# Two small products of a pair-representation kernel moved onto the two 64-row halves of the TensorE array

## The reference, cut to what matters

```python
# layer 0
xn = layernorm(x); left = sigmoid(xn@left1) * (xn@left2); right = sigmoid(xn@right1) * (xn@right2)
p  = layernorm(einsum('nsre,nkre->nske', left, right))
x1 = x + (p^T @ out_w) * sigmoid(xn @ gate)
# layer 1
left  = x1 @ W_left + b_left + x1 @ W_eq + b_eq
rsum  = sum(x1 @ W_right + b_right, axis=2)
o     = left * rsum * sigmoid(x1 @ W_gate + b_gate)
out   = layernorm(o @ W_out + b_out + x1)
```

## Time and profile before

| what | value |
|---|---|
| median of 3 runs | 123.48 us |
| the profiled execution's own time | 123.37 us |
| its span in the trace | 121.6 us |
| PE busy | 93.8 us (77%) |
| weight loads (PEld) busy | 71.7 us (59%) |
| DVE busy | 92.1 us (76%) |
| ACT busy | 73.6 us (61%) |
| POOL busy | 68.9 us (57%) |

### The profile page before, as it was taken

One profiled execution on the slowest core, in us unless ns is written; L12 is line 12 of the kernel. 1 busy time (PEld: TensorE's weight loads), 2 busy tenths in 40 slices (PEclk: granted clock), 3 DMA queues, 4 the chain that ended last, 5 costly groups with the idle time before them and its releaser, 6 DMA issues.

```text
span 121.6 us, 1791 instructions
## 1 busy us (share of the span) xinstructions
PE 93.8 (77%) x566; PEld 71.7 (59%) x566; DVE 92.1 (76%) x222; ACT 73.6 (61%) x129; POOL 68.9 (57%) x81
## 2 busy tenths in 40 slices
PE   1965795199879969999192999999999999697000
PEld 1954353067647759954141559897798879596000
DVE  1079999499988872999999636477498989799920
ACT  2245472976997628994136983645998698761100
POOL 5047679606299001790470397958754797995700
PEclk9999999968999999999998599999999999999755
DMA  2799990000000000000000000000000005429796
GB/s 52 137 147 153 144 129 3 0 0 0 5 0 0 0 3 5 0 3 0 0 0 0 0 0 5 0 0 3 0 0 5 0 0 86 66 35 145 109 145 104
DMA packets 33484, 4.51 MB, mean 37 GB/s; under 512 B 33348, under 2 KB 33476, under 8 KB 33476
## 3 DMA queue, kind: packets, MB, share of 16 engines
q1 hardware_dynamic: 32160, 4.06, 23.9%
q10 hardware_dynamic: 1316, 0.35, 1.4%
HBM read 2.31 MB, written 2.10 MB: 36 GB/s over the span
## 4 chain that ended last, share of the span: by engine, by line
PE 41%; DVE 35%; issue 7%; ACT 7%; DMA 4%; DVEq 0%; SPq 0%
PE bank L878 7%; PE bank L966 6%; DVE acc_p L713 6%; PE bank L1009 5%; PE bank L1018 4%; DMA x_tok<-in_x 4%; DVE lr L613 4%; PE bank L980 3%; PE bank L983 3%; PE bank L981 3%; DVE sums L584 3%; PE bank L939 3%; DVE lr L797 3%; ACT sig_lr L435 2%; DVE st L592 2%
## 5 line engine op out<-in xcount | busy, mean ns | idle before, releaser
L878 PE MATMUL bank<-lr_blk,xnT 64*128 64x256 f32 x128 | 20.1, 451 | 5.6 <-DVE lr L613 4.0
L878 PEld LDWEIGHTS bank<-lr_blk,xnT 64*128 64x128 f32 x128 | 13.3, 211 | 9.9 <-ACT xnT L425 5.4
L613 DVE TENSOR_TENSOR lr<-bank,sig_lr 128x512 f32<-128x512 f32 x16 | 15.8, 1045 | 2.9 <-ACT sig_lr L435 2.6
L363 POOL TENSOR_TENSOR x_low<-x1T,x_high 128x512 fp32r<-128x512 f32 x8 | 11.0, 1373 | 12.2 <-ACT x_high L496 12.1
L355 POOL TENSOR_TENSOR t_tok<-p_sb,rstd 128x512 f32<-128x512 f32 x7 | 10.4, 1489 | 4.9 <-DVE rstd L754 4.9
L414 ACT ACTIVATE std<-st,eps 128x16 f32<-128x16 f32 (+4 forms) x14 | 4.4, 318 | 13.6 <-DVE st L599 5.3
L279 POOL TENSOR_TENSOR xc<-x_tok,sums 128x512 f32<-128x512 f32 (+2 forms) x7 | 8.0, 1145 | 7.4 <-DVE sums L577 7.4
L435 ACT ACTIVATE sig_lr<-bank 128x512 f32<-128x512 f32 x16 | 9.5, 599 | 3.9 <-PE bank L878 3.8
L379 POOL TENSOR_TENSOR sq<-lr,row_rep 128x512 f32<-128x512 f32 x7 | 9.8, 1400 | 2.0 <-DVE lr L800 2.0
L966 PE MATMUL bank<-tT,out_blk 128*128 128x512 f32 x16 | 9.2, 659 | 2.2 <-DVE x1T L771 2.2
L371 POOL TENSOR_TENSOR oT<-o_a,rsum 128x512 f32<-128x512 f32 x8 | 8.7, 1088 | 2.6 <-issue 1.9
(11 more groups left out here) (120 smaller groups left out, 244.1 us busy)
## 6 DMA issues: line engine op xcount, KB each, us to landing
x_tok<-in_x SPq DMA_DIRECT2D x14, 128.0 KB, 4.3
out<-sq SPq DMA_DIRECT2D x7, 256.0 KB, 3.3
x_tok<-in_x SPq DMA_DIRECT2D x4, 64.0 KB, 4.4
w_rep<-in_weights ACTq DMA_DIRECT2D x1, 180.5 KB
out<-sq ACTq DMA_DIRECT2D x1, 128.0 KB, 4.6
out<-sq SPq DMA_DIRECT2D x1, 128.0 KB, 4.9
row_rep<-in_rows ACTq DMA_DIRECT2D x1, 32.0 KB, 5.0
```

Source lines behind the costliest of these rows:

```text
L363: nc.gpsimd.tensor_tensor(x1_low[:, c % 2], x1T[:, c % 3], x1_high[:, c % 2], ALU.subtract).then_inc(x1_low_ready, 1)
L613: nc.vector.tensor_tensor(lr[:, :, s].rearrange("p f s -> p s f"), src[:, :, 2 * CH:4 * CH], sig_lr[:, j % 3].rearrange("p (s f) -> p s f" ...
L878: last = nc.tensor.matmul(dst, xnT[half, c, k * P:(k + 1) * P], lr_blk[half].rearrange("p g m c -> p g (m c)"), start=True, stop=True, ski ...
```

## The change

`centre_y` and `project_y` are cut into halves by rows of the array. Each 128-row call becomes two calls of 64 rows: the upper 64 partitions of the data against the upper left 64 x 64 block of the matrix, and the lower 64 against the lower right one (the other two blocks are zero). The two halves write 64 columns each into two different banks, into the left 256 columns of each bank. So one chunk of y takes half of both banks 6 and 7, and the next chunk takes the same halves: there is one set of banks where there were two. `centre_y(c)` therefore waits until `evacuate_y(c-1)` has finished, where it waited for `evacuate_y(c-2)`. In the loop `centre_y(i-3)` stands behind `project_1(i-2)`, directly ahead of `project_y(i-3)`, where it stood ahead of `project_1(i-2)`. `evacuate_y` reads both banks in each of its two instructions, with the same 512 elements per partition. `project_scaled` is as before.

```diff
+        def y_place(t, j):
+            n, h = divmod(j, 2)
+            return bank[:, Y + t, 0:COLS // 2].rearrange("p (h g n c) -> p h n g c", h=2, g=2, n=2)[:, h, n]
...
             def evacuate_y(c):
                 s = slice(c * SPC, (c + 1) * SPC)
-                src = bank[:, Y + c % 2].rearrange("p (s c) -> p s c", c=CH)
+                src = bank[:, Y:Y + 2, 0:COLS // 2].rearrange("p t (h k) -> p h t k", h=2)
...
             def centre_y(c):
-                b = Y + c % 2
-                if c >= 2:
-                    pe.wait_ge(y_ready, c - 1)
-                elif c == 0:
+                if c:
+                    pe.wait_ge(y_ready, c)
+                else:
                     pe.wait_ge(g_ready, CHUNKS)
                 for j in range(BLK):
                     k = slice(j * P, (j + 1) * P)
-                    nc.tensor.matmul(in_order(bank[:, b], j), x1T[:, c % 3, k], centre_blk[:], start=j == 0, stop=False,
-                                     skip_group_check=True)
+                    for t in range(2):
+                        half = slice(t * P // 2, (t + 1) * P // 2)
+                        nc.tensor.matmul(y_place(t, j), x1T[half, c % 3, k], centre_blk[half, half], start=j == 0,
+                                         stop=False, skip_group_check=True)
 
             def project_y(c):
-                b = Y + c % 2
                 pe.wait_ge(oT_ready, c + 1)
                 for j in range(BLK):
                     k = slice(j * P, (j + 1) * P)
-                    last = nc.tensor.matmul(in_order(bank[:, b], j), oT[:, c % 2, k], wout_blk[:], start=False,
-                                            stop=j == BLK - 1, skip_group_check=True)
+                    for t in range(2):
+                        half = slice(t * P // 2, (t + 1) * P // 2)
+                        last = nc.tensor.matmul(y_place(t, j), oT[half, c % 2, k], wout_blk[half, half], start=False,
+                                                stop=j == BLK - 1, skip_group_check=True)
...
-                if 0 <= i - 3 < CHUNKS:
-                    centre_y(i - 3)
                 if 0 <= i - 2 < CHUNKS:
                     project_1(i - 2)
                 if 0 <= i - 3 < CHUNKS:
+                    centre_y(i - 3)
                     project_y(i - 3)
```

More of the change, by code:

```diff
@@ L512, in evacuate_y @@
                 s = slice(c * SPC, (c + 1) * SPC)
-                src = bank[:, Y + c % 2].rearrange("p (s c) -> p s c", c=CH)
+                src = bank[:, Y:Y + 2, 0:COLS // 2].rearrange("p t (h k) -> p h t k", h=2)
                 act.wait_ge(y_ps, c + 1)
-                nc.scalar.activation(sq[:, s, :], src, ACT.Square).then_inc(ysq_ready, 1)
-                nc.scalar.activation(y[:, s, :], src, ACT.Copy).then_inc(y_ready, 1)
+                nc.scalar.activation(sq[:, s, :].rearrange("p (h t k) c -> p h t (k c)", h=2, t=2), src, ACT.Square
+                                     ).then_inc(ysq_ready, 1)
+                nc.scalar.activation(y[:, s, :].rearrange("p (h t k) c -> p h t (k c)", h=2, t=2), src, ACT.Copy
+                                     ).then_inc(y_ready, 1)
             def root3_of(b):
```

## The result

The changed kernel takes 124.48 us (median of 4 runs, 124.01 to 125.25), the kernel before beside it 123.19 us; the ratio is 1.0095, with a 95% interval of 1.0051 to 1.014. The profiled execution took 124.48 us with a span of 122.7 us, against 123.37 and 121.6. The forecast was 124.5 us. The loss lies under the 1% that the forecast counted as no change; but the interval leaves out 1, so the small loss itself is clear of the noise.

What follows compares the result with a forecast made beforehand. TensorE was taken to bound the kernel until project_1(7) releases gated1(7), then DVE's backlog. 123.37 us plus 1.1 us at gated1(7), other terms nothing, gave 124.5 us; range 122.9 to 125.8.

Steps and rivals of the forecast that it cites:

- The phases: In centre_y and project_y, loading 128 weight columns sets 0.111 us per step, so a phase stays 0.89 us; no gain.
- The changes of size: TensorE going to 64 rows ahead of centre_y and back behind project_y costs 0.30 us net per iteration.
- The order: centre_y behind project_1 frees 0.89 us in iteration 9; with 5 pairs of size changes, gated1(7) comes 1.1 us later.
- The tie with x_low(7): In project_1(7), the third matmul could start at 103.95, x_low(7) ends at 103.96 to 104.26; up to 0.3 us stall.
- hidden changes: Rival: changes of tile size in the loop cost nothing and moving centre_y gains 0.3 us, 123.1 us; chance 0.08.
- The single set: One set of y banks: centre_y's wait for evacuate_y costs nothing in iterations 4 to 8; about 1.2 us wait in chunk 7.
- The ACT rival: Rival: ACT becomes the path, TensorE waiting for evacuate_y in iterations 6 and 8, 125.1 to 125.8 us; chance 0.17.
- This wait costs nothing: Behind the loop, centre_y(7) waits for evacuate_y(6), project_scaled ends at 114.2, ahead of DVE's need at 115.6; no cost.
- the 1.4 us of cover: Behind the loop, the margin between project_scaled ending at 114.2 and DVE wanting it at 115.6.
- Halves twice as fast: Rival: centre_y and project_y steps take 0.056 us; -0.6 x 5, ACT gives back perhaps 1, about 121.0 us; chance 0.07.
- Loads one behind the other: Rival: weight loads of the two halves run in turn, 10 us more in 6 iterations, 135 us; chance 0.03.

Runs made afterwards that it cites:

- Half the streaming: The changed kernel with 32 columns streaming per 64-row matmul in place of 64, half of y left out; ratio to the kernel before 1.0068.
- pair of extra matmuls: Changed kernel with chunk 7 of y in L and G's banks, plus a one-column 128-row matmul between centre_y and project_y (1.0282) or ahead of centre_y (1.015).
- order alone: The kernel before with only centre_y moved behind project_1, 128-row matmuls and two sets of banks kept; ratio to the kernel before 0.9988.
- order and one bank: The kernel before with centre_y behind project_1 and one bank for y in place of two, 128-row matmuls kept; ratio to the kernel before 1.0008.
- quarters: The changed kernel with each 64-row call cut again by 64 columns of the weights, four 64 x 64 tiles; ratio to the kernel before 0.9895.
- extra matmul between: One-column 128-row matmul between centre_y and project_y: first on the changed kernel (126.69 to 129.84 us), then with chunk 7 in L and G (1.0282).
- chunk 7 in L and G: Chunk 7 of y put in the banks of L and G: on the changed kernel ratio 1.0056 to the kernel before, with quarters 0.9848 (121.65 us).

## Why the prediction was right, and where it was not

- **The phases.** 0.89 us for the one without a change of size, steps of 0.11 per half: right, and for the reason given. Half the streaming changed nothing, half the columns of a load nearly halved it.
- **The changes of size.** 0.30 us per iteration forecast and measured: 5.22 against 4.92 us. Two more changes of size cost 0.34 in the pair of extra matmuls.
- **The order.** +1.1 us for `gated1(7)`: 39.21 against 38.12, 1.09. The tie with x_low(7) was one: x_low(7) ended at 103.82, where the third matmul was due, and its step came about 0.2 us late. By the order alone this point came 0.13 earlier, where "hidden changes" had 0.3.
- **The single set.** A wait of 1.2 us in chunk 7 and in no other: it is all that the list of PE's waits has from 71 to 112 us.

```profile
PE bank L1017 <- ACT lr L522: 1.2, 1, 1.2
```

The ACT rival had waits in iterations 6 and 8; there is none, so it fell. "This wait costs nothing" was the step that failed in part: the 1.4 us of cover were reckoned at full clock. In the profiled execution the clock fell to half behind the wait, `project_scaled` took 5.4 us from first start to last end (110.40 to 115.78) in place of 3.7 before, and the cover ended 0.39 us short. The end gave most of it back: L851, the last two sums, took 0.75 us where L844 had taken 1.09, so that the span grew by 1.1 us all the same. With the clock full, the same wait cost nothing (order and one bank).
- **The last two sums.** Before, then changed, with GpSimd's last two products beside them:

```profile
113.06 2.56 POOL L379 TENSOR_TENSOR sq<-lr,row_rep 128x512 f32<-128x512 f32 x2 [1.35 <-DVE lr L800]
115.14 1.09 DVE L844 TENSOR_TENSOR sq<-lr,row_rep 128x256 f32<-128x256 f32 x2
```
```profile
114.11 2.56 POOL L384 TENSOR_TENSOR sq<-lr,row_rep 128x512 f32<-128x512 f32 x2 [1.35 <-DVE lr L807]
116.55 0.75 DVE L851 TENSOR_TENSOR sq<-lr,row_rep 128x256 f32<-128x256 f32 x2
```

Before, the first sum took 0.76 us beside a product that ran until 115.62, the second 0.41; in the changed kernel, where the scaling had waited for PE, the product ended 0.12 us after the sums began and both took 0.42. In all twelve traces it is so: 0.75 us in the four where the last scaling waited for PE, 1.09 or 1.10 in the eight where it did not and the product ran 0.5 us into the sums. So a late last scaling gets some 0.34 us back; that GpSimd's product is what slows the sum fits this but was not tried.
- **The other rivals.** Halves twice as fast: no, 0.89 us. Loads one behind the other: no, 0.30 us for four. The changes hidden: no, 0.15 us stand in the trace at each of the two changes. The terms given for the first of these, -0.6 x 5 and +1 back, make 121.4 us and not the 121.0 stated; nothing hangs on it.
- **The sum.** 124.5 forecast, 124.48 measured; two terms, the 0.39 us and what L851 gave back, were not in it and nearly cancel, by luck. That the totals agree to 0.02 us is luck too: single runs of the changed kernel lie between 124.01 and 125.25 us, and the median of the kernel before was 123.19 us beside it and 123.83 us (29 runs) beside the first experiments. The 1.09 us at `gated1(7)` carry the account, not the totals.
- **What a measurement can tell.** The prediction held that less than about 1% can't be told from no change. Here 0.9% could: the interval of the ratio, 1.0051 to 1.014, leaves out 1.

## What to carry to other kernels

Where data are the weights and a small matrix streams, look first at which of load and stream sets the pace; a matmul with one or eight columns in the same trace tells it. Cutting the rows of a load then brought nothing here, cutting its columns did, and each change of tile size between neighbours on TensorE cost 0.15 to 0.17 us, so halves belong in long stretches of the same size. A wait that is covered at full clock may not be at half clock: reckon the cover with the slower row too.

## What the runs showed of the hardware that I had not expected

Four 64 x 64 tiles run side by side as well as two halves do: two phases of 32 matmuls start 0.51 us apart (80.36 and 80.87), where phases of 16 in halves start 0.94 us apart, with no sign of a limit on issuing them. And with the wait of about 1.2 us ahead of chunk 7 the clock fell to half, during it or up to 2 us behind it, in some profiled executions (the changed kernel, from about 110.4 us on, half the streaming, and the first of the two kernels with an extra matmul between), and stayed full in others (order and one bank, quarters). It was so earlier as well: the 2.2 us that TensorE waits for x1T ahead of `project_q(1)` were followed by half the clock until about 70 us in the kernel before and the changed one, and by full clock in the two kernels with chunk 7 in L and G that have no extra matmul. Which of the two comes was not settled.
